# An AdaLN feed-forward kernel with a per-head mix: the mix as 64x128 products behind up, up and down one step later, an out buffer, and a new order of the last steps

## What is computed

```python
# layer 0
w = L0_cond_weight[ids]                          # (32, 1024, 1024)
c = einsum('bsi,boi->bso', x, w)
x = x + c @ W_base.T + b_base + lora_out(c)      # top-2 of 8 experts, rank 16
# layer 1
W = L1_cond_weights[ids]                         # (32, 64, 64): tokens to tokens
y = einsum('bct,bcd->bdt', x, W)
t = y[..., perm].reshape(-1, 16, 64)             # 16 heads of 64
t = gelu(einsum('bhd,hdm->bhm', t, up))          # 64 -> 256
t = einsum('bhm,hmd->bhd', t, down)              # 256 -> 64
x = x + t[..., unperm]
```

## Time and profile before

| | |
|---|---|
| time, median of 3 runs | 631.04 us (630.94 to 631.26) |
| profiled execution, its own time | 630.16 us |
| its span, first to last instruction | 628.3 us |
| PE busy (matmul records) | 605.7 us, 96% |
| DVE busy | 420.2 us, 67% |
| ACT, POOL busy | 22%, 21% |
| second stage, from its first base product | about 286 to 628 us |
| one ordinary step of the second stage | 10.42 us |

### The profile page before, as it was taken

The page is one execution under the profiler, slowest core; times in us unless marked ns, Lnnn a source line. Parts: engine busy times, 40 slices in busy tenths (PEclk is TensorE's granted clock), DMA queues, the critical chain, the costliest instruction groups (busy, mean ns, idle before and its releaser), DMA issues.

```text
span 628.3 us, 12954 instructions
## 1 busy us (share of the span) xinstructions
PE 605.7 (96%) x4215; PEld 358.6 (57%) x4216; DVE 420.2 (67%) x1194; ACT 139.4 (22%) x267; POOL 134.6 (21%) x192
## 2 busy tenths in 40 slices
PE   3899999999999999999999999999999999999995
PEld 2434444444444444447676767676766666666662
DVE  2026666666666666698777796767976769776762
ACT  2210000000000000044423442323432326232323
POOL 5000000111111110051032232222322223222222
PEclk9899999999999999999999999999999999999999
DMA  8999881188988888821022222222132222222221
GB/s 281 411 408 387 299 294 61 32 282 303 301 300 307 306 295 294 309 59 59 26 68 80 83 69 89 79 78 79 51 99 75 79 77 77 75 75 75 76 76 59
DMA packets 42273, 102.69 MB, mean 163 GB/s; under 512 B 8322, under 2 KB 17538, under 8 KB 42242
## 3 DMA queue, kind: packets, MB, share of 16 engines
q1 hardware_dynamic: 29762, 71.85, 33.9%
q0 software_dynamic: 6784, 21.51, 9.5%
q10 hardware_dynamic: 5696, 8.95, 4.2%
HBM read 93.89 MB, written 8.39 MB: 163 GB/s over the span
## 4 chain that ended last, share of the span: by engine, by line
PE 90%; SPq 3%; DMA 3%; DVE 2%; issue 1%; ACT 0%; DVEq 0%; POOL 0%; ACTq 0%; POOLq 0%
PE wide L421 33%; PE bank L508 18%; PE bank L575 10%; PE bank L516 9%; PE wide L564 8%; PE y_wide L437 4%; PE y_wide L548 3%; SPq L242 3%; DMA ring<-adapters_dram 2%; PE bank L529 1%; PE bank L528 1%; PE bank L532 1%; DVE c_lo L971 1%; PE bank L445 0%; DMA my_id<-ids_dram 0%
## 5 line engine op out<-in xcount | busy, mean ns | idle before, releaser
L421 PE MATMUL wide<-ring,x_in 128*64 128x512 f32 x1024 | 226.4, 597 | 3.7 <-DMA ring<-adapters_dram 3.7
L421 PEld LDWEIGHTS wide<-ring,x_in 128*64 128x64 f32 x1024 | 86.3, 138 | 128.4 <-issue 128.4
L1008 DVE STREAM_TRANSPOSE x_tok<-xres 32x128 f32<-32x128 f32 x480 | 145.1, 302 | 6.1
L862 DVE STREAM_TRANSPOSE c_pair<-wide 32x256 f32<-32x256 f32 x240 | 107.0, 446 | 62.2 <-issue 35.0
L508 PE MATMUL bank<-c_hi,base_t 128*128 128x512 f32 x512 | 140.1, 397 | 0.0
L508 PEld LDWEIGHTS bank<-c_hi,base_t 128*128 128x128 f32 x512 | 93.5, 188 | 29.1 <-issue 11.0
L736 ACT ACTIVATE act_sb<-wide 128x512 f32<-128x512 f32 x128 | 66.2, 605 | 80.2 <-PE wide L564 80.2
L516 PE MATMUL bank<-c_lo,base_t 128*128 (+1 forms) x256 | 78.1, 390 | 0.1
L374 POOL DMA_INDIRECT out_dram<-xres,row_out x32 | 36.7, 1148 | 183.6 <-DVE xres L1000 183.6
L354 POOL COPY c_all<-c_pair 128x512 f32 x30 | 19.3, 670 | 223.8 <-DVE c_pair L862 223.8
L575 PE MATMUL bank<-act_sb,down_sb 128*64 128x512 f32 x256 | 62.0, 605 | 1.0 <-ACT act_sb L736 1.0
(11 more groups left out here) (109 smaller groups left out, 424.3 us busy)
## 6 DMA issues: line engine op xcount, KB each, us to landing
ring<-adapters_dram SPq DMA_DIRECT2D x120, 512.0 KB, 5.3
x_in<-x_seq_dram ACTq DMA_DIRECT2D x32, 256.0 KB, 4.4
up_raw<-up_dram SPq DMA_DIRECT2D x64, 64.0 KB, 2.3
down_sb<-down_dram SPq DMA_DIRECT2D x32, 128.0 KB, 2.6
ar_sb<-lora_a_router_dram ACTq DMA_DIRECT2D x1, 544.0 KB, 4.1
mix_sb<-mix_dram SPq DMA_DIRECT2D x32, 16.0 KB
xres<-xT_dram,row_in POOLq DMA_INDIRECT x32, 3.8
out_dram<-xres,row_out POOLq DMA_INDIRECT x32, 3.0
```

The source lines that it names most:

```text
L421: last = pe.matmul(acc[half][h][z * TOK:(z + 1) * TOK, :], x_in[:, half, z, k, :], ring[:, k, z, h * HALF:(h + 1) * HALF], start=(k == 0), ...
L862: last = nc.vector.transpose(c_pair[r * SQ:(r + 1) * SQ, :, q * SQ:(q + 1) * SQ], wide[half][q * SQ:(q + 1) * SQ, :, :] .rearrange("p h (k ...
L1008: last = nc.vector.transpose(x1_tok[q * SQ:(q + 1) * SQ, :].rearrange("p (c f) -> p c f", f=P)[:, :, f * SQ:(f + 1) * SQ], xres[f * SQ:(f ...
```

## The change

- `mix_tokens` writes 8 products instead of 16: both heads of the block in one weight load of 128 columns (64 rows), so that each sequence of a pair uses a row half of the array.
- In a step PE now runs base and lora of j, down of j-3, up of j-2, and mix of j-1 behind it. Up and down of a block are thus one step later than before.
- `result` writes into a new buffer `out_sb`, and POOL gathers the next x into `xres` before it stores `out_sb`; in the last four steps it writes into `xres` as before. One semaphore counts all stores.
- The order on DVE and ACT follows: DVE takes `layer0_out` first, then `result`, `x1_turned`, `up_rest`, `y_rest`. `x1_turned` now also waits for the mix before it (`y_done`). The splits of the next group's c and of hw are moved.
- The last step has buffers of its own (`act_last`, `x1_last`, `y_hi_last`, `y_lo_last`, bank 4 for the last down) and its own order (`last_steps`).

Ahead of these rows stand now `layer0_out` of the step and two c_lo products, so that all four c_lo products lie between x1 and its transposes; before, three of them lay ahead of x1. The core of the diff (what moves on ACT for the early steps, and renamed arguments, are left out):

```diff
@@ -92,7 +92,14 @@
 
         c_hi = at(split_at, "c_hi", [P, KT, GT], F32R)
         b_hi = at(split_at + 4 * 4096, "b_hi", [P, KT, P], F32R)
-        hw_hi = at(split_at + 5 * 4096, "hw_hi", [P, GT], F32R)
+        hw_hi = at(split_at + 5 * 4096, "hw_hi", [P, 2 * GT], F32R)
...
 
+        def late(g, j, n):
+
+            return isinstance(g, int) and g * STEPS + j >= LAST - n
...
+
+            def finish(g, j):
+
+
+
+                b, nj = j % XBUF, (j + XBUF) % STEPS
                 next_row(row_out, row_out_step, j, g * STEPS + j)
+                refills = not late(g, j, XBUF)
+                if refills:
+                    next_row(row_in, row_in_step, nj, g * STEPS + j + XBUF)
                 pool.wait_ge(fin_ok, g * STEPS + j + 1)
                 on_its_own()
-                pool.indirect_dma_start(out_rows, bass.IndirectOffsetOnAxis(ap=row_out[:, j:j + 1], axis=0),
-                                        xres[:, j % XBUF, :], None).then_inc(stored[j % XBUF], 16)
-
...
+                store(g, j, out_sb[:, :] if refills else xres[:, b, :])
 
             with pool.Fori(0, GROUPS - 1) as g:
                 for j in range(STEPS):
-                    store(g, j)
...
+
+
 
                 pe.wait_ge(x1_tok_ok, g * STEPS + j + 1)
                 if j == 0:
@@ -544,18 +573,19 @@
                 pe.sem_inc(mix_begun, 1)
                 for p in range(GP):
                     for z in range(2):
-                        for h in range(2):
-                            last = pe.matmul(y_wide[h * HD:(h + 1) * HD, z, p * TOK:(p + 1) * TOK],
-                                             x1_tok[z * TOK:(z + 1) * TOK, p * P + h * HD:p * P + (h + 1) * HD],
-                                             mix_now[z * TOK:(z + 1) * TOK, p, :], start=True, stop=True,
-                                             skip_group_check=True)
+                        rows = slice(z * TOK, (z + 1) * TOK)
+                        last = pe.matmul(y_wide[:, z, p * TOK:(p + 1) * TOK], x1_tok[rows, p * P:(p + 1) * P],
+                                         mix_now[rows, p, :], start=True, stop=True, skip_group_check=True)
                 last.then_inc(y_done, 1)
 
...
             def down_heads(g, j):
                 pe.wait_ge(down_in[j % 2], (g * (STEPS // 2) + j // 2 + 1) * 16)
-                pe.wait_ge(fin_ok, g * STEPS + j)
+                if not late(g, j, 1):
...
                 lora(0, 2)
+                up_heads(0, 0)
                 mix_tokens(0, 1)
-                pe.wait_ge(x1_ok, 2)
-                down_heads(0, 0)
-                up_heads(0, 1)
+
+            def last_steps():
+
+
+
+
+                g = GROUPS - 1
+                up_heads(g, 5)
+                mix_tokens(g, 6)
+                pe.wait_ge(x1_ok, LAST)
+                to_tokens(7, last_d_ps)
+                down_heads(g, 4)
+                pe.wait_ge(y_ok, LAST - 1)
+                mix_tokens(g, 7, x1_last)
+                up_heads(g, 6)
+                down_heads(g, 5)
+                up_heads(g, 7)
+                down_heads(g, 6)
+                down_heads(g, 7)
 
...
                 for part in range(CS):
                     base(g, j, part)
                 lora(g, j)
+                if late(g, j, 1):
+                    last_steps()
+                    return
+                down_heads(g3, j3)
+                up_heads(g2, j2)
                 mix_tokens(g1, j1)
-                down_heads(g2, j2)
-                up_heads(g1, j1)
 
             over_steps(pe, step, 6)
...
-                    up_leading(g, j)
+                if late(g, j, 1):
+                    x1_tokens(1, x1_last, last_d_ps)
+                gelu(g2, j2, 2)
+                gelu(g2, j2, 3)
+                up_leading(g1, j1)
+                if j == 5 and not late(g, j, STEPS):
+                    hw_leading(g + 1)
 
             over_steps(act, step)
             y_leading(GROUPS - 1, STEPS - 1)
+            for i in range(4):
+                gelu(GROUPS - 1, STEPS - 2, i)
+            up_leading(GROUPS - 1, STEPS - 1)
             for i in range(4):
                 gelu(GROUPS - 1, STEPS - 1, i)
...
             def result(g, j):
-                b = j % XBUF
-                dve.wait_ge(d_done, g * STEPS + j + 1)
-                nc.vector.tensor_tensor(xres[:, b, :], d_ps[:, :], xres[:, b, :], ALU.add).then_inc(fin_ok, 1)
+
+
+                b, n = j % XBUF, g * STEPS + j
+                to = xres[:, b, :] if late(g, j, XBUF) else out_sb[:, :]
+                dve.wait_ge(d_done, n + 1)
+                if early(g, j, 1):
+                    dve.wait_ge(base_ok, 7)
+                elif not late(g, j, XBUF):
+                    dve.wait_ge(stored, n * 16)
+                nc.vector.tensor_tensor(to, d_bank(g, j)[:, :], xres[:, b, :], ALU.add).then_inc(fin_ok, 1)
 
             def x1_turned(g, j):
 
                 b = j % XBUF
                 dve.wait_ge(x1_ok, g * STEPS + j + 1)
...
-                    hw_rest(g)
+                layer0_out(g, j)
+                if early(g, j, 2):
+                    up_rest(g1, j1)
+                    y_rest(g1, j1)
+                    x1_turned(g, j)
+                    return
+                if late(g, j, 1):
+                    y_rest(g1, j1)
+                    up_rest(g1, j1)
+                    result(g3, j3)
+                    return
+                if j == STEPS - 1:
+                    c_rest(g + 1, 0)
+                    c_rest(g + 1, 1)
+                    result(g3, j3)
+                    c_rest(g + 1, 2)
+                    up_rest(g1, j1)
+                    y_rest(g1, j1)
+                    c_rest(g + 1, 3)
+                    x1_turned(g, j)
+                    return
                 if not early(g, j, 3):
                     result(g3, j3)
+                x1_turned(g, j)
                 up_rest(g1, j1)
-                if early(g, j, 5) and j >= 3:
-                    base_rest(SPLIT_ORDER[j + 3])
-                splits = j == STEPS - 1 and not (isinstance(g, int) and g == GROUPS - 1)
-                if splits:
-                    for part in range(CS - 1):
-                        c_rest(g + 1, part)
-                layer0_out(g, j)
                 y_rest(g1, j1)
-                if splits:
-                    c_rest(g + 1, CS - 1)
-                if not (isinstance(g, int) and g == GROUPS - 1 and j == STEPS - 1):
-                    x1_turned(g, j)
+                if early(g, j, 4):
+                    base_rest(SPLIT_ORDER[j + 4])
+                if j == 5 and not late(g, j, STEPS):
+                    hw_rest(g + 1)
 
             over_steps(dve, step, 5)
+            y_rest(GROUPS - 1, STEPS - 1)
+            up_rest(GROUPS - 1, STEPS - 1)
```

More of the change, by code:

```diff
@@ L173, in build @@
         xres_in = [sem(f"xres_in{i}") for i in range(XBUF)]
-        stored = [sem(f"stored{i}") for i in range(XBUF)]
+        stored = sem("stored")
         down_in = [sem(f"down_in{i}") for i in range(2)]
@@ L221, in early, with act_of, d_bank, y_split @@
             return isinstance(g, int) and g * STEPS + j < n
+        def late(g, j, n):
+            return isinstance(g, int) and g * STEPS + j >= LAST - n
+        def act_of(g, j):
+            return act_last if late(g, j, 3) and j % 2 == 1 else act_sb
+        def d_bank(g, j):
+            return last_d_ps if late(g, j, 1) else d_ps
+        def y_split(g, j):
+            return (y_hi_last, y_lo_last) if late(g, j, 1) else (y_hi, y_lo)
+        def hw_slot(g):
+            return bass.ds((g % 2) * GT, GT)
         block = ctx.enter_context(nc.Block(no_gpsimd_drain=True))
@@ L533, in lora, with to_tokens, mix_tokens @@
                           start=False, stop=True).then_inc(c_done, 1)
-            def to_tokens(j):
-                transposes([tr_ps], [xres[:, j % XBUF, p * P:(p + 1) * P] for p in range(GP)], tr_done)
-            def mix_tokens(g, j):
+            def to_tokens(j, ps):
+                transposes([ps], [xres[:, j % XBUF, p * P:(p + 1) * P] for p in range(GP)], tr_done)
+            def mix_tokens(g, j, x1_tok=x1_tok):
                 pe.wait_ge(x1_tok_ok, g * STEPS + j + 1)
@@ L731, in hw_leading, with x1_tokens @@
             def hw_leading(g):
[L732 removed]
+                nc.scalar.copy(hw_hi[:, hw_slot(g)], hw_t[:, bass.ds(g * GT, GT)]).then_inc(hw_hi_ok, 1)
             def gelu(g, j, i):
                 act.wait_ge(u_done, (g * STEPS + j) * 2 + i // 2 + 1)
[L736 to L738 removed]
+                nc.scalar.activation(act_of(g, j)[:, i, :], u_ps[i][:, :], ACT.Gelu).then_inc(act_ok, 1)
+            def x1_tokens(way, x1_tok, ps):
                 act.wait_ge(tr_done, way + 1)
[L740 removed]
+                nc.scalar.copy(x1_tok[:, :], ps[:, :]).then_inc(x1_tok_ok, 1)
             def up_leading(g, j):
@@ L772, in step @@
                     return
-                if j == 0:
-                    act.wait_ge(c_done, g * STEPS)
-                    hw_leading(g)
```

(24 more changed lines are left out.)

67 lines of the change are left out of this document (30 added, 37 removed).

## The result

The changed kernel takes 637.72 us (median of 4 runs, 637.22 to 640.5), the kernel before 630.99 beside it (4 runs, 630.69 to 631.26): a ratio of 1.0116, with 95% between 1.0102 and 1.0129. It is slower by 6.7 us. The prediction was 636.0 with 632.5 to 640.

What follows compares the result with a forecast made beforehand. PE's queue was taken as the bound. Ordinary steps +5.9, start +0.4 and end -1.3 made +5.0 us, so 636.0 us, 0.8% slower; range 632.5 to 640, narrower range 634.5 to 637.5 at 0.66.

Steps and rivals of the forecast that it cites:

- What bounds the kernel: In the second stage PE's queue is the bound, 10.42 us a step; DVE, ACT and the transfers are slack.
- The mix after, the term that decides: Each of the mix's eight pairs takes as long as its load of 128 columns, 0.112 us; lower bound 0.06.
- An entry less: In a step the mix's first load hides under up's last pair, saving one change of form, 0.14 us.
- The third rival: The mix's first load isn't hidden behind up's last pair: 0.11 us more, 31 times, +3.3, 639.3; chance 0.10.
- The ordinary step, +0.21: From the last lora product to base: 4.39 us before, 4.60 after; +0.21 a step, 5.9 us for 28 steps.
- The start, +0.4: First two mixes cost 0.36 us more each, a first load 0.05; 0.20 and 0.14 are saved; together +0.4.
- The end, -1.3: PE's waits of 0.93 and 1.04 us go, a new one of 0.5 comes, last two mixes add 0.72; -1.3 taken.
- at nothing: DVE, POOL and SP were counted as adding no time; POOL and SP issue what they issued.
- A cheap wide load: Rival: a load of 128 columns costs no more than a narrow one, pairs stay at 0.06 us: 624.2; chance 0.12.
- the number of products: Rival: the count of products sets the mix's time, giving the same time as the cheap load; chance inside its 0.12.
- DVE at a group's end: Rival: DVE's transposes, counted at 13.9 us against 14.3 wanted by the mix, come 1 us late three times: 639; 0.05.

Runs made afterwards that it cites:

- e3: The changed kernel with every mix except the very first streaming 32 columns instead of 64, same weight loads: 637.13 us, ratio 1.0102 to the kernel before.
- e3b: The changed kernel with every product of the mix streaming 128 columns instead of 64, same weight loads: 639.83 us, ratio 1.0145 to the kernel before.
- e2: The kernel before with only its mix as eight products of 64x128, at its old place between lora and down: 644.35 us, ratio 1.0213.
- e5: The quarter mix kernel (e1) with row numbers of the last store counted before the store ahead of it is issued: 630.83 us against 631.20, ratio 1.0006.
- e1: The changed kernel with the mix again as 16 products of 64x64 in quarters, at its new place behind up: 631.41 us against 630.81, ratio 1.0008.
- e7: The quarter mix kernel (e1) with each store of a refilled step held until the transposes of x1 are done: 632.55 us, ratio 1.0024.

## Why the prediction was right, point by point

The mechanism held, and the effect came out a third larger than forecast: +6.7 us instead of +5.0. The time of 637.72 lies in the stated range, but 0.2 above the narrower one of 634.5 to 637.5 that was given 0.66.

- **What bounds the kernel.** Right: PE's queue before and after. DVE, ACT and POOL all changed places in the step, DVE waits for the mix in a new place, and no ordinary step has a wait of PE.
- **The mix after, the term that decides.** Right: 0.111 us a pair against 0.112. The size came from up's loads, 0.11 apart; the choice between 0.11 and 0.06 rested on the sort's loads of 128 columns (304 ns against 218 for 64) and not on the transposes (140 ns). There was some luck in that choice. The 304 is a mean of two loads (281 and 328 ns) at 4 us, and the clock of 0.52 was read for 18 to 22 us; for 3.5 to 5 us the same view gives 1.00. That the sort ran at the slow level too is only made likely by the transposes, 223 ns at 7.4 to 11 us and 221 in the slow stretch. The changed kernel has the clean pair: 187 ns against 134 at full clock. e3 and e3b show that the load sets the pace, e2 that the width by itself costs 0.41 a step. The Trainium skill (TensorE: Matmul & The Clock Gate, section "LDWEIGHTS (loading the stationary operand)") prices a load by its columns at 1.2 GHz, an estimated 0.107 us for 128; the pairs come 0.111 apart, so the trace agrees.
- **An entry less.** Right: the first pair starts 0.23 behind up's last, as announced, and not 0.34. The third rival is false.
- **The ordinary step, +0.21.** The mechanism is right, the size was short by 0.04: 10.673 against 10.63. The terms that were mis-sized are those left at their old value: up's 1.25 from its first load to its last pair is 1.29, and from base's first product to the last lora product it is 6.05 (609.29 to 615.34 at the end of the trace) instead of 6.02 (604.28 to 610.30); the mix gives 0.02 back. 28 times 0.04 is 1.2 us, most of the 1.7 by which the time lies above the forecast; the start has 0.1 of it and the end 0.4.
- **The start, +0.4.** Measured +0.54.
- **The end, -1.3.** Measured -0.89. PE's wait is even smaller than said (0.34, not 0.5). What was missed is that I counted POOL "at nothing": "POOL and SP issue what they issued". They do, but POOL's row numbers for the last store are counted after the store before it, and with the two last results nearer to each other this comes to stand on the path: 0.5 us. e5 takes it away in the profile of the quarter mix, 0.56.
- **The rivals.** A cheap wide load, or the number of products, would have given pairs of 0.06 and about 624; the pairs are at 0.111. DVE at a group's end: it is ready 0.61 us before the mix, where 0.4 was counted, and those steps are as long as the others. The Trainium skill (TensorEngine Tiling (Array Packing), section "Instruction Overhead") has some 60 cycles for each product. Counted one behind the other at 2.4 GHz that is an estimated 0.8 us for 32; e1's 32 records fit in 0.62 us, so the trace doesn't agree with that sum for products in quarters, which run side by side. Halving the products didn't pay here.
- **Still open.** Why the products of 512 columns behind a change of form take longer to settle at 0.227 us apart in the new order. Behind its first spacing base has four spacings of 0.228 to 0.236 in before, nine of 0.224 to 0.236 in the changed kernel and ten of up to 0.240 in e1, and each of the three rows ends in the same values. e1 shows that it comes with the order and not with the width; e7 shows that it is neither POOL's store nor its gather. One step of e1 (base at 424.39) gives a hint: there base starts 0.08 later behind the mix than elsewhere, and its second run takes 0.91 again, with gather and store beside it as in the others. No run shows what it is.

## What to carry to other kernels

Before merging small products into wider ones, compare what a product streams with what it loads: once the load of the stationary operand is longer than the stream, fewer and wider products aren't cheaper. Here four quarters load 64 columns each at the same time, 0.06 us a group, and two halves 128 each, 0.111 us a pair, for the same 64 streamed columns. Price a load from a row of the same kind (plain products, not transposes) and read the distance between starts, not the length of records. And when an end is shortened, look at every queue behind it: what was counted at nothing in the middle comes to stand on the path there.

## What the hardware showed that I had not expected

- The products right behind a change of form are slower for a while, and the order of the forms decides for how long: four base products and two lows behind them are as before (1.13 and 0.46), but the next four take 0.93 instead of 0.91, and in up 12 take 1.60 instead of 1.58. In the kernel with the old order and the wide mix (e2) up is 1.58 again.
- A record of a product in the mix is 272 or 273 ns long for 32, 64 and 128 streamed columns alike: it contains the time for which it waits for its weights, 0.09, 0.06 and nothing. Only the first pair, which doesn't wait, shows its stream (187, 213 and 267 ns).
- The end of the unchanged first stage varies by 1.0 us (285.78 to 286.76) over nine profiled executions. In a single profile this is more than most terms of this case, so spans were compared from the first base product on.
